# A graph network's equivariant pass loads its edge features already transposed

## What is computed

```python
def mlp2(x, w1, b1, w2, b2):
    return relu(x @ w1 + b1) @ w2 + b2
wk = mlp2(edge_features, k_w1, k_b1, k_w2, k_b2)      # edge_features: [100000, 64]
wv = mlp2(edge_features, v_w1, v_b1, v_w2, v_b2)
k = tensor_product(x_dst, edge_sh, wk, Cqk)           # w * sum over d,s of x*sh*C
v = tensor_product(x_dst, edge_sh, wv, Cv)
attn = einsum('ehd,ehd->eh', q[edge_src], k)          # softmax of it per node, then
upd = segment_sum(v * alpha[..., None], edge_src)     # the weighted sum of v per node
```

## Time and profile before

| | us |
|---|---|
| median of 3 runs (14642.67 to 14645.07) | 14645.04 |
| span of the profiled execution | 16787.0 |
| TensorE busy in it | 11273.9 |
| GpSimd busy | 8192.1 |
| VectorE busy | 8000.8 |
| ScalarE busy | 4679.8 |

### The profile page before, as it was taken

One profiled execution on the slowest core, in us unless ns is written; L12 is line 12 of the kernel. 1 busy time (PEld: TensorE's weight loads), 2 busy tenths in 40 slices (PEclk: granted clock), 3 DMA queues, 4 the chain that ended last, 5 costly groups with the idle time before them and its releaser, 6 DMA issues. The chain is left out here.

```text
span 16787.0 us, 272571 instructions
## 1 busy us (share of the span) xinstructions
PE 11273.9 (67%) x66979; PEld 9278.5 (55%) x66979; DVE 8000.8 (48%) x26981; ACT 4679.8 (28%) x11796; POOL 8192.1 (49%) x9684
## 2 busy tenths in 40 slices
PE   1666666666666679999999999956667774336333
PEld 1555555555555557777777777755566653333333
DVE  3555545555444446666666666632223332223222
ACT  1555545544455533333333333300001110001000
POOL 0444434444444434444444444356667745663666
PEclk9888878888787779999999999955555566557555
DMA  1111111111111110000000000011111122113111
GB/s 19 39 38 39 40 34 41 39 38 34 40 40 39 40 28 14 13 14 13 14 13 14 13 14 13 11 21 22 22 22 22 21 77 84 22 22 140 23 22 23
DMA packets 457388, 519.18 MB, mean 31 GB/s; under 512 B 213952, under 2 KB 337600, under 8 KB 450490
## 3 DMA queue, kind: packets, MB, share of 16 engines
q0 software_dynamic: 225280, 317.64, 8.9%
q1 hardware_dynamic: 215898, 197.42, 3.7%
q10 hardware_dynamic: 15840, 0.68, 0.1%
HBM read 400.54 MB, written 114.67 MB: 31 GB/s over the span
## 5 line engine op out<-in xcount | busy, mean ns | idle before, releaser
L525 POOL DMA_INDIRECT conv_pass_rows<-kv_rows,conv_pass_stage x2640 | 2509.3, 951 | 1163.2 <-issue 785.6
L1646 PE MATMUL tfn_pass_psA<-tfn_pass_cw,tfn_pass_outerT 128*128 128x256 f32 (+1 forms) x8800 | 2835.3, 413 | 0.0
L1483 POOL TENSOR_TENSOR tfn_pass_outer<-tfn_pass_rows,tfn_pass_sh 128x576 f32<-128x576 f32 x880 | 1071.0, 1245 | 2354.1 <-PE tfn_pass_psR L1568 2354.0
L1100 PE MATMUL segment_rgcn_psO<-segment_rgcn_rows,segment_rgcn_oh 128*128 128x64 f32 x3520 | 856.4, 425 | 1746.6 <-DMA segment_rgcn_rows<-rel_rows,segment_rgcn_stage 1274.3
L525 POOL DMA_INDIRECT segment_sage_rows<-h_rows,segment_sage_stage x1760 | 1750.4, 995 | 511.2 <-issue 449.6
L525 POOL DMA_INDIRECT segment_rgcn_rows<-rel_rows,segment_rgcn_stage x1760 | 1675.8, 952 | 531.7 <-issue 480.5
L1100 PEld LDWEIGHTS segment_rgcn_psO<-segment_rgcn_rows,segment_rgcn_oh 128*128 128x128 f32 x3520 | 783.5, 328 | 1819.4 <-issue 1433.3
L1646 PEld LDWEIGHTS tfn_pass_psA<-tfn_pass_cw,tfn_pass_outerT 128*128 128x128 f32 (+1 forms) x8800 | 1419.2, 193 | 317.0 <-issue 182.0
L1744 DVE CUSTOM_DVE_ANT_0 tfn_pass_junk<-tfn_pass_psB,tfn_pass_outside 128x512 f32<-128x512 f32 x1760 | 1201.5, 690 | 784.2 <-PE tfn_pass_psB L1600 734.8
L749 DVE CUSTOM_DVE_ANT_0 conv_pass_junk<-conv_pass_psB,conv_pass_outside 128x512 f32<-128x512 f32 x1100 | 725.3, 690 | 1293.5 <-PE conv_pass_psB L659 843.9
L634 PE MATMUL conv_pass_at_node<-conv_pass_top_new,conv_pass_ohT 128*128 128x128 f32 x5280 | 964.1, 338 | 415.4 <-DVE conv_pass_top_new L756 322.9
(11 more groups left out here) (316 smaller groups left out, 22346.0 us busy)
## 6 DMA issues: line engine op xcount, KB each, us to landing
rel_rows<-rgcn_tables_y SPq DMA_DIRECT2D x50, 2080.0 KB, 6.3
conv_pass_rows<-kv_rows,conv_pass_stage POOLq DMA_INDIRECT x2640
conv_pass_ea<-in_edge_attr SPq DMA_DIRECT2D x660, 64.0 KB
tfn_pass_ef<-in_edge_attr SPq DMA_DIRECT2D x220, 128.0 KB
segment_sage_rows<-h_rows,segment_sage_stage POOLq DMA_INDIRECT x1760
segment_rgcn_rows<-rel_rows,segment_rgcn_stage POOLq DMA_INDIRECT x1760
tfn_pass_rows<-h_rows,tfn_pass_stage POOLq DMA_INDIRECT x880
kv_rows<-conv_tables_kv SPq DMA_DIRECT2D x18, 256.0 KB, 2.3
```

Source lines behind the costliest of these rows:

```text
L525: pool.indirect_dma_start(rows[:, s, j, :], None, table, bass.IndirectOffsetOnAxis(ap=stage[:, s, j:j + 1], axis=0)).then_inc(landed[s], 16)
L1100: mm = nc.tensor.matmul(psO[s % 2][:, 0:D], oh[:, s, j, :], rows[:, s, j, :], start=(j == 0), stop=(j == SUB - 1))
L1483: ins = pool.tensor_tensor(outer[:, s % 2, j, :, :], rows[:, s, j, :].unsqueeze(1).to_broadcast(full), sh[:, s % 2, j, :].unsqueeze(2).to_ ...
L1646: mm = nc.tensor.matmul(psA[j // 2][:, j % 2, :], outerT[0:r, s % 2, kb, e:e + P], cw[0:r, kb, :], start=(kb == 0), stop=(kb == KB - 1))
```

## The change

The host passes a second copy of the edge features, transposed: 64 rows of 100000. The pass loads 512 columns of it straight into `efT`, which now has two buffers, in 64 rows of 2 KB. The four transposes, ScalarE's copy and the buffer `ef` go. Since the columns of the loaded tile stand in the edges' order `4p + j` while the rest of the pass wants all edges of place 0 first, then place 1 and so on, the hidden layer reads its moving operand in steps of four floats. It waits for the load's semaphore itself, SyncE's next load waits for `hid_ready` where it waited for `f_ready`, and the turned logits and the first transposes of outer no longer wait for `efT_ready`.

```diff
+def turned_load(sp, b, flag, name, g, buf, sem):
+
+    _, _, ordered, _, _ = next(a for a in b.edge_arrays if a[0] == name)
+    first = sp.value_load(b.start[0:1, ds(g, 1)], min_val=0, max_val=E - GE)
+    with sp.If(flag == 0):
+        sp.dma_start(buf, b.turned[name][:, ds(first, GE)]).then_inc(sem, 16)
+    with sp.Else():
+        sp.dma_start(buf, ordered[ds(first, GE), :].rearrange("e w -> w e")).then_inc(sem, 16)
...
-        ef = ph.sb("ef", [P, 2, SUB, D])
...
-        efT = ph.sb("efT", [D, GE])
+        efT = ph.sb("efT", [D, 2, GE])
...
-                    at_least(sp, f_ready, g - 1)
+                    at_least(sp, hid_ready, g - 1)
                     sp.sem_inc(slot_turn, 1)
-                    edge_load(sp, b, flag, "a64", g, ef[:, s % 2, :, :].rearrange("p j w -> p (j w)"), ef_in[s % 2])
+                    turned_load(sp, b, flag, "a64", g, efT[:, s % 2, :], ef_in[s % 2])
...
-                    def features():
-                        g, _, s = hot
-                        emptied(1)
-                        pe.wait_ge(ef_in[s % 2], pair_in(hot))
-                        pe.sem_inc(pe_turn, 1)
-                        for j in range(SUB):
-                            mm = nc.tensor.transpose(odd[0:D, j * P:(j + 1) * P], ef[:, s % 2, j, :], b.eye[:, :])
-                        mm.then_inc(f_ready, 1)
...
                     def turn_logits():
                         g, _, _ = here
-                        if hot:
-                            pe.wait_ge(efT_ready, hot[0] + 1)
-                        elif product:
+                        if product:
                             emptied(1)
...
                     def hidden():
-                        g, _, _ = hot
-                        pe.wait_ge(efT_ready, g + 1)
+                        g, _, s = hot
+                        pe.wait_ge(ef_in[s % 2], pair_in(hot))
...
-                        nc.tensor.matmul(even[:, :], w1[:, :], efT[:, :], start=True, stop=True).then_inc(hid_ready, 1)
+                        pe.sem_inc(pe_turn, 1)
+                        of = efT[:, s % 2, :].rearrange("d (p j) -> d j p", j=SUB)
+                        nc.tensor.matmul(even[:, :].rearrange("h (j p) -> h j p", j=SUB), w1[:, :], of, start=True, stop=True).then_inc(hid_ready, 1)
...
-                        else:
-                            pe.wait_ge(efT_ready, g + 1)
+                        elif product:
+                            emptied(1)
...
-                        between[1].append(features)
...
-                        act.wait_ge(f_ready, g + 1)
-                        nc.scalar.activation(efT[:, :], odd[0:D, :], ACT.Copy).then_inc(efT_ready, 1)
...
+    b.turned = {"a64": ins["edge_attr_64T"]}
...
+    a["edge_attr_64T"] = a["edge_attr_64"].T
```

More of the change, by code:

```diff
@@ L1414, in tfn_pass_phase @@
         names = ("loaded", "zeroed", "turn", "staged", "slot_turn", "dve_turn", "pe_turn", "eye_ready", "picks_in", "pick_ready", "oh_ready",
-                 "oh_f_ready", "outer_ready", "outer_turned", "t_ready", "ohT_ready", "outside_ready", "q_here_ready", "q_ready", "f_ready",
-                 "efT_ready", "hid_ready", "hidT_ready", "o_turned", "outerT_ready", "w_ready", "w_added", "product_ready", "keys_ready", "vals_ready",
+                 "oh_f_ready", "outer_ready", "outer_turned", "t_ready", "ohT_ready", "outside_ready", "q_here_ready", "q_ready", "hid_ready", "hidT_ready", "o_turned", "outerT_ready", "w_ready", "w_added", "product_ready", "keys_ready", "vals_ready",
                  "matched", "alpha_ready", "part_step", "parts_ready", "pT_ps", "pT_ready", "spread", "max_done", "top_ready", "fall_ready",
@@ L1419, in tfn_pass_phase @@
         (loaded, zeroed, turn, staged, slot_turn, dve_turn, pe_turn, eye_ready, picks_in, pick_ready, oh_ready,
-         oh_f_ready, outer_ready, outer_turned, t_ready, ohT_ready, outside_ready, q_here_ready, q_ready, f_ready,
-         efT_ready, hid_ready, hidT_ready, o_turned, outerT_ready, w_ready, w_added, product_ready, keys_ready, vals_ready,
+         oh_f_ready, outer_ready, outer_turned, t_ready, ohT_ready, outside_ready, q_here_ready, q_ready, hid_ready, hidT_ready, o_turned, outerT_ready, w_ready, w_added, product_ready, keys_ready, vals_ready,
          matched, alpha_ready, part_step, parts_ready, pT_ps, pT_ready, spread, max_done, top_ready, fall_ready,
```

## The result

The changed kernel takes 14827.8 us (median of 4 runs, 14819.4 to 14832.5) where the kernel before takes 14644.0: 184 us more, 1.0121 times as long (95% interval 1.0109 to 1.0133). The forecast was 14640, and the range ended at 14796. The likeliest case was wrong; the stride rival (14796) named the mechanism and priced it 32 us too low.

What follows compares the result with a forecast made beforehand. In the equivariant pass VectorE, with ScalarE's `outside` close beside it, was taken to set the time up to the hidden layer, despite TensorE's 94.6% busy. Terms summed to -5 us + 0, from 14645 to 14640 us; range 14570 to 14796.

Steps and rivals of the forecast that it cites:

- The likeliest case: Whole kernel: no measurable change, 14640 us, chance 0.58.
- the stride rival: Hidden layer slowed by its strided read, up to 0.69 us a group, 151 us, giving 14796 us; chance 0.21.
- The four transposes stood in a wait: TensorE before the node maxima: removing 0.43 us a group, at most 95 us, gains nothing because ScalarE's `outside` is awaited.
- TensorE is the bound: Rival, equivariant pass: the transposes' 0.43 us a group come back whole, 95 us faster, 14550 us; chance 0.15.
- ScalarE's copy: nothing: Dropping ScalarE's feature copy, 0.58 us a group and 128 us in all, gains nothing; ScalarE next waits for the turned logits.
- The turned logits' second wait, 0 to 15 us, 5 taken: Turn of the logits no longer waits for efT: 0 to 0.07 us a group gained, low third taken.
- The stride: between 0 and 0.69 us a group, 0 taken: Hidden layer reading four floats a step: upper bound 151 us from a VectorE read, none taken, its present pace being slow.
- The load: nothing: Feature load of 64 rows of 2 KB for 128 of 1 KB: same 128 KB, needed over 40 us later, no cost.
- SyncE's queue: nothing: SyncE waiting for the hidden layer delays the load of `sh` by 4.7 us, leaving 4.3 us; no cost.
- the clock pays: Rival, behind VectorE's loop return: the low-clock stretch doubles, 62 us slower, 14707 us; chance 0.04.
- a good witness for this pass: The traced execution, 16787 us against the runs' 14645, was held reliable for the equivariant pass, poor for the last phases.

Runs made afterwards that it cites:

- e17: The kernel before with one edit, SyncE's load of the edge features waiting for the hidden layer; 0.9974 of the kernel before on a slow chip.
- e18: The changed kernel with a contiguous read and ScalarE's relu writing hidT in steps, all of the reference computed; 0.9943 of the kernel before on a slow chip.
- e16: The kernel before with only the hidden layer's read of efT made strided, four floats a step, on a quick chip; 1.0122 of the kernel before, 176 us slower.
- e15: The kernel before, unchanged, profiled on a quick chip; 14663 us, 20.99 us a group.
- e1: The changed kernel with the hidden layer reading efT contiguously (order of edges changed), on a slow chip; 0.9939 of the kernel before.
- e8: The changed kernel with the hidden layer reading efT contiguously (order of edges changed), on a quick chip; 14602.6 us, 0.9965 of the kernel before.
- e7: The changed kernel itself, run again on a quick chip; 14830.9 us, 1.0122 of the kernel before.
- e11: The changed kernel with the hidden layer reading in steps of eight floats; a single execution of 16816 us, the kernel before 16778.
- e4: The changed kernel with a contiguous read and ScalarE's relu writing hidT in steps, on a quick chip; 14607.2 us, 0.9968 of the kernel before.
- e3: The changed kernel with the hidden layer reading in steps of two floats instead of four, on a slow chip; 0.9926 of the kernel before.
- e2: The kernel before with only the hidden layer's read of efT made strided, four floats a step, on a slow chip; 1.0062 of the kernel before.
- e6: The changed kernel with a contiguous read and the second layer's weight loads reading hidT in steps of four floats; 14621.3 us, 0.9981 of the kernel before.
- e13: The kernel before, unchanged, profiled again on a slow chip; no total time of its own is given.

## Why the prediction was wrong

By the steps of the change:

1. *The four transposes stood in a wait.* Right for the stretch that I argued about. With them the hidden layer's weight load starts 24.40 - 20.91 = 3.49 us behind that of the one-hots, without them 8.19 - 4.75 = 3.44, and TensorE's idle time in front of L1525 took their place. The rival "TensorE is the bound" (14550) falls: only 0.05 of the 0.43 us came back in the groups without a loop return, the contiguous variant ended at 14603, and it has e17's shorter wait at the loop's return. Further down the group it was not the whole story on slow chips, as e18 against e17 shows (46 us).
2. *ScalarE's copy: nothing.* Nothing in the runs contradicts it, though no run takes out the copy alone.
3. *The turned logits' second wait, 0 to 15 us, 5 taken.* It can't be told apart from step 1: L1536 still starts 0.11 us behind `parts` where it was 0.12.
4. *The stride: between 0 and 0.69 us a group, 0 taken.* This is the step that failed, and it makes the result. Measured: 0.80 us a group by the stride alone (176 us, e16 against e15), 0.86 by the records. The reason I gave for taking 0 was that the layer's pace of 1.0 ns a column was slow enough that an element is asked for only every second cycle. The runs show that the pace bears steps of two floats (0.71 us a record) and not of four (1.09). The upper end was short as well: 1.68 ns a column was VectorE's price, and the nearest row of another engine is no bound. Measured are 1.92 us for 1024 columns, 1.88 ns each.
5. *The load: nothing.* Its shape, right as far as the runs show: e16 has the old load and the ratio of the changed kernel, 1.0122, and e1 and e8 have the new one and are faster than the kernel before.
6. *SyncE's queue: nothing.* Wrong, in the other direction. I asked whether the later load would come too late. It comes in good time, but I did not ask whom the earlier one had disturbed: it met VectorE's wait at the loop's return. Worth 52 us in e17. That VectorE fetches instructions there, as I wrote in the expectation, is a guess; the profile names no cause (`issue`).

In the changed kernel the gain of step 6 does not show in the time: it has the late load and the ratio of the stride alone, 1.0122. The granted clock of its pass is 0.96 and that of e16's 0.97 (below). The clock records of the traces say it more finely: in the pass the clock is at its lower level, 1.2 GHz, for 429 us in the changed kernel and 400 in e7, against 312 in e16 and 274 in e8. The added stretches, 14 in the changed kernel, begin 4.8 to 5.0 us into the group behind a loop's return, while the strided hidden layer is at work; TensorE has had no idle time of the loop's kind just before them. At the 27% that the prediction worked out for low clock, 117 us more of it are worth 31 us by estimate, the greater part of the some 45 us that are missing. So the rival "the clock pays" (0.04) came true in part, beside the stride. It takes both changes on a quick chip: e16, e8 and, on a slow chip, e11 (303 us) don't have it.

```profile
4771.00:9539.00 4768.00, 4564.56 (x28534) 3327.16 (x28535) 3138.75 (x9550) 1390.11 (x2833) 1932.85 (x1967) 0.96 0.06 13
```
```profile
4772.00:9543.00 4771.00, 4616.68 (x29409) 3382.66 (x29408) 3141.91 (x9550) 1496.11 (x3056) 1937.62 (x1971) 0.97 0.06 13
```

Last, I called the traced execution a good witness for this pass although it was 2142 us longer than the timed ones. It was not: a group takes 20.99 us in the timed kind, 21.45 in the one I read, and the difference is a wait that hides about half of the stride (94 us where 176 were paid without it).

## What to carry to other kernels

A reordering read is not free because it moves no more bytes: when a transpose is saved by reading its source in steps, put the steps on an engine that nobody waits for, as e4 does, and keep the steps of an fp32 moving operand at two elements or fewer. When a profile's span does not match the timed runs, read it as that of another machine and look for waits that only it has. And when a load moves in time, ask which engine's wait or transfer it now leaves alone, not only whether it still comes in time.

## What was not expected of the hardware

- An fp32 moving operand of 64 x 512 takes 0.66 to 0.70 us a record when it is contiguous, 0.71 in steps of two floats (e3), and 1.09 to 1.11 in steps of four and eight. At the lower clock the stride costs almost nothing: 2.15 us strided and 2.08 contiguous for the two records, at full clock 1.94 and 1.02 (e16, e15). The Trainium skill says in "Advanced Engine Details and Errata", section Memory Cachelines, that two hits on a 16-byte line are needed and that a new line each time is penalised; these four strides agree with it. The Trainium skill also counts a stride of four fp32 elements as free ("SBUF — State Buffer", section Door 1); e2 and e16 do not agree with that, and the measurement decides.
- Steps of four floats cost a weight load of 128 columns 0.13 us (190 to 323 ns, e6). ScalarE's write of 512 columns in steps of 128 floats costs it 0.46 us (687 to 1147 ns, e4).
- A load of 128 KB issued while VectorE stands at its loop's return lengthens that wait from 131.8 to 149.1 us in 52 times, 0.33 us each (e17 against e13, both on slow chips). With the load moved the whole run is 52 us shorter, of which this wait is 17.
- Runs in different places differ by 14% on this kernel (14650 against 16770 us), and the pass at hand differs by a wait of 0.65 us in most groups: VectorE's first maximum starts up to 1.3 us later there. What makes it is open.
